# SiLU of a dense expert layer as g/2 (1 + tanh(g/2)), its product moved to VectorE

## What is computed

```python
hg = jnp.einsum('ecd,efd->ecf', expert_in, w_gate)
hu = jnp.einsum('ecd,efd->ecf', expert_in, w_up)
expert_out = jnp.einsum('ecf,edf->ecd', jax.nn.silu(hg) * hu, w_down)
...
shared_out = jnp.einsum('bsef,edf->bsd', jax.nn.silu(hg) * hu, shared_w_down)
shared_out = shared_out / shared_w_gate.shape[0]
```

## Time and profile before

| | us |
|---|---|
| median of three runs | 5571.4 |
| lowest and highest | 5562.84, 5574.16 |
| span of the profiled execution, first to last instruction | 5548.6 |
| third stage in it | about 4018 to 5548.6 |
| one image with tiles in the third stage | about 101 |

### The profile page before, as it was taken

The page is one execution under the profiler, slowest core; times in us unless marked ns, Lnnn a source line. Parts: engine busy times, 40 slices in busy tenths (PEclk is TensorE's granted clock), DMA queues, the critical chain, the costliest instruction groups (busy, mean ns, idle before and its releaser), DMA issues.

```text
span 5548.6 us, 81822 instructions
## 1 busy us (share of the span) xinstructions
PE 4842.2 (87%) x25633; PEld 2616.5 (47%) x25633; DVE 3586.2 (65%) x7699; ACT 2987.7 (54%) x5420; POOL 1021.9 (18%) x1348
## 2 busy tenths in 40 slices
PE   5888888888888886957888888888899999999999
PEld 1222222222222221336777877787755555555554
DVE  6677777777777762555665656555576676766765
ACT  2655565665655653414555555556755455455552
POOL 2212112121222112202333333333210000000000
PEclk7999999999999998979999999999999999999999
DMA  2522222222222211223545454544321111111112
GB/s 84 144 70 81 81 70 70 70 73 78 73 89 82 66 45 38 29 68 106 165 140 163 141 162 147 157 146 129 106 61 45 50 48 45 50 46 47 52 45 75
DMA packets 406297, 477.10 MB, mean 86 GB/s; under 512 B 87640, under 2 KB 249648, under 8 KB 403760
## 3 DMA queue, kind: packets, MB, share of 16 engines
q1 hardware_dynamic: 372128, 424.84, 25.4%
q0 software_dynamic: 20576, 35.55, 2.3%
q10 hardware_dynamic: 13168, 11.48, 0.8%
HBM read 308.54 MB, written 145.57 MB: 82 GB/s over the span
## 4 chain that ended last, share of the span: by engine, by line
PE 33%; DVE 15%; issue 3%; DVEq 3%; ACT 2%; ACTq 0%; SPq 0%; DMA 0%
PE n_ps_f L2153 4%; PE n_ps_f L2146 4%; PE n_ps_xy L1801 3%; PE n_ps_h L1791 3%; PE n_ps_c L2193 2%; PE n_ps_h L2205 2%; PE n_ps_f L2140 2%; PE n_ps_f L1649 2%; PE n_ps_xy L2209 1%; DVEq L2025 1%; DVE n_stats L971 1%; DVE n_xln L983 1%; PE n_ps_f L995 1%; PE n_ps_h L2209 1%; DVE n_down_weights L2024 1%
## 5 line engine op out<-in xcount | busy, mean ns | idle before, releaser
L597 ACT ACTIVATE a_probs<-ps_b 128x512 f32<-128x512 f32 x2048 | 1111.0, 594 | 794.8 <-PE ps_b L693 782.0
L454 DVE TENSOR_REDUCE a_negmax<-ps_a 128x1 f32<-128x1024 f32 x1024 | 1206.1, 1219 | 378.9 <-PE ps_a L637 369.3
L637 PE MATMUL ps_a<-a_k_stack,a_q_stack 96*128 96x512 bf16 x2048 | 634.6, 396 | 178.8 <-DVE a_negmax L454 89.9
L693 PE MATMUL ps_b<-a_q_stack,a_k_stack 99*128 99x512 bf16 x2048 | 673.6, 391 | 68.2 <-ACT a_probs L597 30.9
L1604 ACT ACTIVATE n_hidden<-n_ps_h,n_b 128x128 f32<-128x128 f32 x1472 | 420.2, 374 | 339.1 <-PE n_ps_h L1791 338.3
L706 PE MATMUL ps_o<-a_probs,a_v_ones 128*32 128x512 f32 x4096 | 562.0, 622 | 0.2 <-ACT a_probs L597 0.2
L637 PEld LDWEIGHTS ps_a<-a_k_stack,a_q_stack 96*128 96x128 bf16 x2048 | 146.1, 99 | 732.2 <-DVE a_negmax L454 468.9
L1801 PE MATMUL n_ps_xy<-n_down_weights,n_hidden 128*128 x2944 | 410.7, 284 | 78.9 <-ACT n_xy L1618 72.8
L693 PEld LDWEIGHTS ps_b<-a_q_stack,a_k_stack 99*128 99x128 bf16 x2048 | 196.2, 100 | 487.8 <-ACT a_probs L597 251.5
L1801 PEld LDWEIGHTS n_ps_xy<-n_down_weights,n_hidden 128*128 128x128 f32 x2944 | 369.1, 196 | 117.0 <-issue 112.8
L1791 PE MATMUL n_ps_h<-n_xy,n_up_weights 128*128 128x128 f32 x2944 | 399.8, 279 | 3.6 <-issue 1.8
(11 more groups left out here) (346 smaller groups left out, 7532.8 us busy)
## 6 DMA issues: line engine op xcount, KB each, us to landing
n_up_weights<-in_L_ffn_W_dram SPq DMA_DIRECT2D x368, 256.0 KB, 2.7
n_up_weights<-score_scratch SPq DMA_DIRECT2D x512, 128.0 KB, 2.9
split_scratch<-a_pieces SPq DMA_DIRECT2D x180, 256.0 KB
a_q_stack<-split_scratch SPq DMA_DIRECT2D x128, 192.0 KB, 3.7
a_k_stack<-split_scratch SPq DMA_DIRECT2D x128, 192.0 KB, 4.1
rows_scratch<-n_zero SPq DMA_DIRECT2D x16, 1472.0 KB, 10.5
outs_scratch<-n_xy SPq DMA_DIRECT2D x176, 128.0 KB, 1.9
n_xg<-rows_scratch SPq DMA_DIRECT2D x80, 256.0 KB
```

Source lines behind the costliest of these rows:

```text
L454: dve.tensor_reduce(negmax[:, b, t:t + 1], bank, axis=AX.X, op=ALU.max, negate=True).then_inc(ring_read, 1)
L597: act.activation(probs[:, m % PROBS, 512 * k:512 * k + 512], ps_b[:, k, :], ACT.Exp).then_inc(b_exp, 1)
L637: last = pe.matmul(bank[:, cols], q_stack[0:KS, h, 128 * t:128 * t + 128], k_stack[0:KS, h, cols], start=True, stop=True)
L693: pe.matmul(ps_b[:, k, :], k_stack[:, h, 128 * t:128 * t + 128], q_stack[:, h, 512 * k:512 * k + 512], start=True, stop=True).then_inc(b_u ...
```

## The change

The SiLU is no longer one activation. ScalarE takes tanh(g/2) of the gate bank into `act_up`, and copies g itself into a new pair of buffers, `gates` (memory that the second stage used for its own ranking). Both come from the same bank, and one semaphore, renamed `tanh_up`, follows the copy. VectorE then forms (tanh + 1) times g in SBUF, followed by a drain, ahead of its wait for the up product. The result is twice the SiLU. The factor is made good in the scores (0.5 in L2075) and for the shared pair in its own factor (0.25 for 0.5). Nothing is changed in DMAs, in TensorE's instructions or in the slots.

```diff
+                 gates=[gate["above"][:, :, :].rearrange("p a f -> p (a f)"), gate["same"][:, :, :].rearrange("p a f -> p (a f)")],
...
-                    dve.wait_ge(silu_up, i * STEPS + n + 1)
+                    dve.wait_ge(tanh_up, i * STEPS + n + 1)
+                    dve.scalar_tensor_tensor(act_up[:, n % 2, :], act_up[:, n % 2, :], 1.0, gates[n % 2], ALU.add, ALU.mult)
+                    dve.drain()
                     dve.wait_ge(u_ps, i * STEPS + n + 1)
                     if unit < PAIRS:
                         dve.tensor_tensor(act_up[:, n % 2, :], act_up[:, n % 2, :], ps_u[n % 2][:, :], ALU.mult).then_inc(u_read, 1)
                         dve.drain()
                     else:
-                        dve.scalar_tensor_tensor(mixed[(i * STEPS + n) % 3], act_up[:, n % 2, :], 0.5, ps_u[n % 2][:, :], ALU.mult, ALU.mult).then_inc(u_read, 1)
+                        dve.scalar_tensor_tensor(mixed[(i * STEPS + n) % 3], act_up[:, n % 2, :], 0.25, ps_u[n % 2][:, :], ALU.mult, ALU.mult).then_inc(u_read, 1)
...
-            act.activation(score_t[:, :], pb[0:E, :], ACT.Copy).then_inc(S["st_up"], 1)
+            act.activation(score_t[:, :], pb[0:E, :], ACT.Copy, scale=0.5).then_inc(S["st_up"], 1)
...
-                    act.activation(act_up[:, n % 2, :], ps_g[:, :], ACT.Silu).then_inc(silu_up, 1)
+                    act.activation(act_up[:, n % 2, :], ps_g[:, :], ACT.Tanh, scale=0.5)
+                    act.activation(gates[n % 2], ps_g[:, :], ACT.Copy).then_inc(tanh_up, 1)
...
                     if n:
-                        pe.wait_ge(silu_up, i * STEPS + n)
+                        pe.wait_ge(tanh_up, i * STEPS + n)
                     pe.matmul(ps_g[:, :], wg(unit), xt2(i)[:, cols], start=True, stop=True).then_inc(g_ps, 1)
```

More of the change, by code:

```diff
@@ L1873, in dense_attention_and_silu @@
     wg, wu, wd = (lambda unit, n=n, x=x: shared[x][:, unit, :] if unit < PAIRS else shared_units[n] for n, x in enumerate(("wg", "wu", "wd")))
-    scores, act_up, mixed, result = (shared[x] for x in "scores act_up mixed result".split())
+    scores, act_up, mixed, result, gates = (shared[x] for x in "scores act_up mixed result gates".split())
     pa, pb, ps_g, ps_u, ps_o = banks
@@ L1879, in dense_attention_and_silu @@
     attention_in, choice_in, ffn_in, result_ps, result_up = (sem(x) for x in "attention_in choice_in ffn_in result_ps result_up".split())
-    g_ps, u_ps, silu_up, u_read, mixed_up, score_stored = (sem(x) for x in "g_ps u_ps silu_up u_read mixed_up score_stored".split())
+    g_ps, u_ps, tanh_up, u_read, mixed_up, score_stored = (sem(x) for x in "g_ps u_ps tanh_up u_read mixed_up score_stored".split())
     scores_in = [sem(f"scores_in{n}") for n in range(RING)]
```

## The result

The changed kernel takes 5680.6 us (median of 4 runs, 5679.1 to 5689.6), the kernel before, beside it, 5567.1 us. The ratio is 1.0209, with 1.0194 to 1.0223 as its 95% interval. The forecast of 5668 us is 12.6 us short, and inside its range; its difference of 96.4 us met 113.5 us. The profiled execution has a span of 5678.3 us, 129.7 over that of before.

What follows compares the result with a forecast made beforehand. TensorE was taken to bound an image's tile part, VectorE's order of work the part between; a walk of one image gave 6.55 us, +96.4 us in all: span 5645.0, plus 22.8 outside it, 5667.8 us, range 5620 to 5715.

Steps and rivals of the forecast that it cites:

- the loads went: Third stage, ScalarE: all 255 table loads vanish; the rival that they stay had 0.08, +19 us, 5687 us.
- the tiles hid their products: Attention tiles: 0.78 us fits in VectorE's 0.83 us wait; the rival without cover had 0.10, 44 us, 5711 us.
- nothing was absorbed: Two rivals: half absorbed, 5610 us, chance 0.06; full absorption in VectorE's idle time, 5560 to 5575 us, chance 0.06.
- image's end, units 14 to 17: VectorE without idle time: four products of 0.78 us, less 0.36 us free before TensorE, +2.76 us an image.
- next image's start, to unit 3's gate: Unit 1's product +0.78, table load gone -1.29, second activation +0.60, drain 0.12: +0.21 us an image.
- units 2 to 4, to the first turning: Up to TensorE's first transposes: three products, 2.34 us, less 0.41 us of VectorE waiting, +1.93 us an image.
- units 5 and 6, to the second: Up to the second transposes: two products, 1.56 us, less 0.69 us free, +0.87 us an image.
- unit 8, to the fourth: Product ahead of eight small additions, where TensorE already waits for the sum: +0.78 us an image.
- The product's price: VectorE's new product with its drain: 0.78 us a unit, bounds 0.6 and 0.83, from a 688 ns product.
- The faster rival: Image's start: ScalarE's load, not VectorE's queue, ends TensorE's 3.47 us stall; 52 us won, 5519 us, chance 0.08.
- the clock at 1.2 GHz: TensorE slowed behind new stalls of 3.7 and 2.2 us: 0.5 to 0.8 us an image, up to 11 us.
- The images without tiles: The fifteenth image pays six products of 0.78 us, 4.7 us; the last image pays nothing.

Runs made afterwards that it cites:

- e4: Kernel before, SiLU and its loads kept, plus ScalarE's copy of g behind it, which nothing reads: 5565.2 us, ratio 1.0018 to before.
- e1: Kernel before with Tanh in place of SiLU, without the copy of g and without VectorE's product: 5567.7 us, ratio 1.0016 to before.
- e12: Changed kernel plus four TensorE matmuls ahead of its wait for a tile series' first Exp, images 2 and on: 5653.6 us, ratio 1.0169 to before.
- e3: Kernel before, SiLU and loads kept, plus a VectorE instruction of the product's size and a drain, result unchanged: 5680.2 us, ratio 1.0219 to before.
- e5: Changed kernel with VectorE's new product left out in units 7 and 9 to 13, kept in the other 12: 5676.6 us, ratio 1.0206 to before.
- e2: Changed kernel without VectorE's new product and its drain, Tanh and copy kept: 5556.6 us, ratio 1.0001 to before.

## Why the prediction was right

The sign, the size and the place were as forecast, and each rival fell: the loads went, the tiles hid their products, nothing was absorbed. Point by point, by the walk's own terms, in us an image:

| step | forecast | measured |
|---|---|---|
| image's end, units 14 to 17 | +2.76 | +2.66 |
| next image's start, to unit 3's gate | +0.21 | -0.01 |
| units 2 to 4, to the first turning | +1.93 | +2.53 |
| units 5 and 6, to the second | +0.87 | +2.11 |
| unit 8, to the fourth | +0.78 | +0.86 |
| the tiles behind it | 0 | +0.10 |
| sum | +6.55 | +8.25 |

- **The product's price.** 0.78 us with its drain, 0.76 measured. Forecast from another product by its shape, it held.
- **The image's start.** The copy alone costs 0.48 (e4), Tanh without loads gives 1.42 back (e1), and the product takes up the rest. The faster rival needed ScalarE to decide here. It does decide when unit 3's gate product starts, but what it gives is lost by the first and second turning.
- **Mis-sized: units 5 and 6.** The queue's part is right (7.73 in e12 against a walk of 7.88). The rest, 1.62 us (1.4 net, as said above), is the clock at 1.2 GHz behind a stall of 2.4 to 4.0 us; before had 0.23 us of it in the mean (7.24 against 7.01). The prediction had it as 0.5 to 0.8 us, in the range and not in the sum. It should have stood in the sum: the two images of before with a stall of 2.7 us there already showed 8.44 and 8.49 us to the second turning, against 7.01. The prediction compared whole images (101.80 against 101.26), which hid two thirds of it: the image of 101.26 us was slower in three other pieces (16.36 against 15.87 us to the first turning, 14.82 against 14.49 to the fourth, 14.06 against 13.92 to unit 3's gate).
- **Mis-sized: units 2 to 4.** The walk took off 0.41 us of VectorE's idleness, read in an image whose TensorE was slow there (16.36 us for this piece; seven of the thirteen have 15.86 or 15.87). In after every image has 18.58. From 15.86 that is +2.72, and three products with their drains are 2.28, which is what e3 with its loads in place shows (18.16). The other 0.4 us is a part of the load's gain that didn't pass on. In before and in e3 VectorE waits for ScalarE at unit 2 and starts together with unit 3's gate matmul (of e3_product_alone):

```profile
4260.04 0.69 DVE L2022 SCALAR_TENSOR_TENSOR n_down_weights<-n_down_weights 128x512 f32<-128x512 f32 x1 [0.66 <-ACT n_down_weights L2092]
...
4260.06 1.70 PE L2207 MATMUL n_ps_h<-n_v,n_tok_next 128*128 128x512 f32 x2 [4.05 <-ACT n_down_weights L2092]
```

  In after the gate matmul starts at 4261.71, but VectorE has its product by the scores (L2034) until 4261.97 and comes to the new product at 4262.11, 0.40 us behind, in every one of the thirteen images. The walk booked the 0.69 us that ScalarE gives as won for all that follows; between e3 and after 0.79 us are won at the gate matmul, and 0.37 are left at the first turning.
- **The images without tiles.** The fifteenth got 5.2 us longer (4.7 forecast), the last one 1.9 where I had nothing. Its first units in the kernel after:

```profile
5626.43 1.12 PE L2209 MATMUL n_ps_h<-n_down_weights,n_tok_next 128*128 128x512 f32 x2 [0.32 <-ACT n_gate_above L2094]
...
5628.73 1.12 PE L2209 MATMUL n_ps_h<-n_down_weights,n_tok_next 128*128 128x512 f32 x2 [0.32 <-ACT n_gate_same L2094]
```

  In the first units, where no down product stands between, a gate product came 1.7 to 1.8 us behind the last in before (5496.40, 5498.11, 5499.93), and matmul, Tanh and copy don't fit: it is 2.2 to 2.3 us now. The earlier trace rows showed a unit with its down product. Another 0.5 us is at the image's half, where TensorE waits 0.81 us for ScalarE's L2083, and 0.32 in before.
- **The sum.** Thirteen images by 8.25 are 107.2, the first has 7.3, the fifteenth 5.2, the last 1.9: 121.6 us in the profiled executions. The other 8.0 us of their difference lie ahead of the third stage, which the change doesn't touch, and belong to these two executions. The medians differ by 113.5 us. The prediction added the 22.8 us by which the median lay over the span; in after a median of 5680.6 us stands beside a span of 5678.3 us, so a profiled execution is no fixed distance from the median. The profiled execution of after took 5680.15 us, 1.85 more than its span; most of the 22.8 us is thus taken to be a difference between executions of before. The forecast's 96.4 us has 113.5 us of the medians beside it, and 121.6 us in the stage where it was walked.

## What to carry to other kernels

Count an engine's free time where the added instruction will stand: VectorE was idle 32 us of each image's 101, and an instruction of 0.76 us in twelve places of eighteen cost 8.0 us an image (e5 against e2), where twelve times its price are 9.1, while in the other six it cost 0.03. A table load that runs while its engine waits costs nothing here; taking away 254 of them, 326 us of ScalarE's work, was worth nothing by itself and 0.2% with TensorE kept busy in the stall, and the instruction that replaced them on the engine with the full queue cost 2.2%. Where TensorE stalls, price the stall with the slow time that follows it, from a stretch of the same trace in which it shows.

## What the runs showed of the hardware

- Shortening a stall can move the fall of the clock to a place where it costs more. In before the 3.3 to 3.7 us stall ahead of unit 3's gate product usually brought the clock to 1.2 GHz where VectorE's queue covered it (two pieces in 2.07 us), and in the two images where full speed lasted there (1.13 us) it fell at the first turning instead (8.44 and 8.49 us to the second, in place of 7.01). e1 shortened the first stall, and lost 1.35 us behind the second.
- Two matmuls whose result nobody reads made e1 0.4% faster (1.0016 to 0.9978).
- GpSimd and VectorE, each with two fp32 operands in SBUF, shut each other out for whole instructions: GpSimd's 1157 ns became 1457 and 1658 on average, and a VectorE step of 2.29 us (L1023) 3.35.
